# The values product of an attention block: three split passes per group, or 32-column strips in plain float32 for two groups at once

## The reference, cut to what matters

```python
q, k, v = ln(x) @ Wq.T + bq, ctx @ Wk.T + bk, ctx @ Wv.T + bv     # heads of 32 columns
scores = einsum('bhnd,bhmd->bhnm', q, k) / sqrt(32)
o = einsum('bhnm,bhmd->bhnd', softmax(scores), v)                 # the product that is changed
x = x + tanh(g_xattn) * (o @ Wo.T + bo)
h = ln(x) @ W1 + b1
act = relu(h + c * w_imag * sin(phase + 0.1 * h))                 # c: a constant per column
x = x + tanh(g_ffn) * (act @ W2 + b2)
```

## Time and profile before

| | |
|---|---|
| runs | 2210.45 us median (2209.47 to 2213.6) |
| the profiled execution, first to last instruction | 2210.9 us |
| PE busy in matmuls | 2162.8 us (98%), 10129 matmuls |
| values product in PE | 576 matmuls, 144.7 us busy |
| DVE, ACT, POOL busy | 66%, 55%, 18% |
| granted PE clock, mean of the span | 0.996 |

### The profile page before, as it was taken

One profiled execution on the slowest core, in us unless ns is written; L12 is line 12 of the kernel. 1 busy time (PEld: TensorE's weight loads), 2 busy tenths in 40 slices (PEclk: granted clock), 3 DMA queues, 4 the chain that ended last, 5 costly groups with the idle time before them and its releaser, 6 DMA issues.

```text
span 2210.9 us, 28991 instructions
## 1 busy us (share of the span) xinstructions
PE 2162.8 (98%) x10129; PEld 1797.9 (81%) x10129; DVE 1448.6 (66%) x2533; ACT 1212.1 (55%) x3571; POOL 403.2 (18%) x331
## 2 busy tenths in 40 slices
PE   8889999999999989999999999999999999999999
PEld 6778888888888867888888888888888888888887
DVE  4567776776776758656656666566566566665654
ACT  3477777777777746444454444444444444544443
POOL 4033433333343321101101001011011010010110
PEclk9989999999999999999999999999999999999999
DMA  7534444545544534313123123123131231231210
GB/s 225 184 70 116 109 106 112 130 103 111 128 106 109 128 129 115 77 50 65 59 56 77 58 58 76 58 39 76 42 74 57 58 77 58 58 77 58 39 39 19
DMA packets 402479, 186.92 MB, mean 85 GB/s; under 512 B 324292, under 2 KB 338985, under 8 KB 402335
## 3 DMA queue, kind: packets, MB, share of 16 engines
q1 hardware_dynamic: 400943, 184.41, 33.3%
q0 software_dynamic: 960, 0.64, 0.2%
q10 hardware_dynamic: 432, 0.04, 0.0%
HBM read 108.86 MB, written 59.38 MB: 76 GB/s over the span
## 4 chain that ended last, share of the span: by engine, by line
PE 61%; DVE 2%; ACT 1%; DMA 0%; issue 0%; ACTq 0%; DVEq 0%
PE pair_bank L56 30%; PE m_bank L56 30%; DVE w_split L1429 0%; DVE hidden L1463 0%; DVE turns L1459 0%; DMA w_chunk<-in_L_ffn_W_dram 0%; ACT relu L1389 0%; DVE sine L1456 0%; ACT hidden L1398 0%; ACT turns L1400 0%; DVE relu L1446 0%; DVE stats L180 0%; DVE x_in L205 0%; ACT sine L1405 0%; ACT w_split L1385 0%
## 5 line engine op out<-in xcount | busy, mean ns | idle before, releaser
L56 PE MATMUL pair_bank<-w_split,relu 128*128 128x512 f32 x3072 | 738.5, 389 | 4.6 <-DVE relu L1446 4.0
L56 PE MATMUL m_bank<-xT,w_split 128*128 128x512 f32 x3024 | 726.3, 389 | 0.0
L56 PEld LDWEIGHTS pair_bank<-w_split,relu 128*128 128x128 f32 x3072 | 576.3, 188 | 126.5 <-issue 4.8
L56 PEld LDWEIGHTS m_bank<-xT,w_split 128*128 128x128 f32 x3024 | 567.8, 188 | 117.6
L1405 ACT ACTIVATE sine<-turns 128x512 f32<-128x512 f32 x256 | 162.0, 633 | 393.7 <-DVE turns L1459 393.7
L1052 ACT ACTIVATE exps<-pair_bank,lowest 128x77 f32<-128x77 f32 x1024 | 318.7, 361 | 81.5 <-DVE lowest L1102 81.5
L1389 ACT ACTIVATE relu<-hidden 128x512 fp32r<-128x512 f32 x256 | 162.2, 633 | 329.7 <-PE m_bank L56 228.6
L1446 DVE SCALAR_TENSOR_TENSOR relu<-hidden,relu 128x512 fp32r<-128x512 f32 x256 | 181.5, 709 | 201.2 <-ACT relu L1389 201.2
L1463 DVE SCALAR_TENSOR_TENSOR hidden<-sine,sine_gain,hidden 128x512 f32<-128x512 f32 x256 | 197.0, 770 | 170.1 <-ACT sine L1405 170.1
L200 POOL TENSOR_TENSOR rstd<-var_eps,minus_half 128x4 f32<-128x4 f32 x32 | 38.3, 1196 | 1154.8 <-DVE var_eps L196 1154.8
L1052 ACT ACTIVATION_READ_ACCUMULATOR exps<-pair_bank,lowest 128x1 f32 x1024 | 248.6, 243 | 0.0
(11 more groups left out here) (123 smaller groups left out, 1896.2 us busy)
## 6 DMA issues: line engine op xcount, KB each, us to landing
x_in<-in_x_dram SPq DMA_DIRECT2D x16, 1024.0 KB, 5.5
residual<-in_x_dram SPq DMA_DIRECT2D x64, 256.0 KB, 2.8
xT<-x_in SPq DMA_DIRECT2D x256, 64.0 KB, 2.3
x_scratch<-residual SPq DMA_DIRECT2D x64, 256.0 KB, 2.4
x_in<-x_scratch SPq DMA_DIRECT2D x16, 1024.0 KB, 5.5
residual<-x_scratch SPq DMA_DIRECT2D x64, 256.0 KB, 3.6
out_dram<-residual SPq DMA_DIRECT2D x64, 256.0 KB, 2.1
quad_scratch<-x_in SPq DMA_DIRECT2D x60, 256.0 KB, 5.6
```

Source lines behind the costliest of these rows:

```text
L56: mm = pe.matmul(out, stationary(s), moving(m), start=first and n == 0, stop=last and n == len(PASSES) - 1)
```

## The change

The values product no longer uses hi and lo. The values are stored and loaded once, as float32. A transposed chunk of probabilities is copied by DVE alone into one float32 tile. Each head gets its own matmul: weights are the 128 x 32 columns of `v_diag` that belong to the head in that chunk, and the result goes to the head's own 32 partitions of the bank. A head's 77 rows fall into one or two chunks; over two groups every head has exactly three such pieces (`strips`). `value_products` issues the 12 pieces of two groups, step by step, the four heads in turn, at the end of the odd slots; the even slots have no values product. Operands are plain float32.

In the compiled program of the changed kernel each plain float32 piece stands as two pairs of a weight load and a matmul, one pair right behind the other (384 pieces, 768 matmuls; the 576 split ones are gone).

```diff
-        v_diag = sb(att, "v_diag", [P, 2, G // 2, 2, NC, P], F32R)
+        v_diag = sb(att, "v_diag", [P, 2, G // 2, NC, P])
...
+        for j in range(HG):
+            strip = []
+            for second in range(2):
+                of_head = [c for h, c, _, _, _ in pieces[second] if h == j]
+                strip += [(second, c, i == 0, i == len(of_head) - 1) for i, c in enumerate(of_head)]
+            strips.append(strip)
...
-                        sp.wait_ge(v_split, RT * r + j + 1)
+                        sp.wait_ge(v_summed, RT * r + j + 1)
...
-                    if not s.values_first:
-                        s.values = (*m.next(), h.next()[0]) if s.finish else None
+                    if s.finish and g % 2 == 1 and not s.values_first:
+                        s.values = [(*m.next(), h.next()[0]) for _ in range(2)]
...
-                        if s.finish and place != AFTER and g < 2:
-                            sp.wait_ge(m_full, s.values[0])
-                            load_values(sp, b, g, values_loaded[g])
+                        if s.values and place != AFTER and g == 1:
+                            sp.wait_ge(m_full, s.values[1][0])
+                            for second in range(2):
+                                load_values(sp, b, second, values_loaded[second])
...
-                    pe.wait_ge(m_split, n - 2)
-                    for c in range(NC):
-                        mm = matmul3(pe, m_bank[bank][:, :], lambda p: v_diag[:, g % 2, g // 2, p, c, :],
-                                     lambda p: probsT[p][:, g % 2 * (NC - 1) + c, :], c == 0, c == NC - 1)
-                    mm.then_inc(m_full, 1)
+                    pe.wait_ge(m_split, ns[1] - 2)
+                    for step in range(len(strips[0])):
+                        for j in range(HG):
+                            second, c, first, last = strips[j][step]
+                            mm = pe.matmul(m_bank[banks[second]][j * DH:(j + 1) * DH, :],
+                                           v_diag[:, second, pair, c, j * DH:(j + 1) * DH],
+                                           probsT[:, second * (NC - 1) + c, :], start=first, stop=last)
+                            if (step, j) in (ends[0], ends[1]):
+                                mm.then_inc(m_full, 1)
...
-                        if s.finish:
-                            for c in s.chunks:
-                                bank_hi(probsT[0][:, c, :], *s.probs[c])
...
-                def bank_lo(dst, hi, n, bank):
-                    dve.wait_ge(t_hi, n)
-                    dve.tensor_tensor(dst, t_bank[bank][:, :], hi.bitcast(F32), ALU.subtract).then_inc(t_split, 1)
+                def copy_probs(c, n, bank):
+                    dve.wait_ge(t_full, n)
+                    dve.tensor_copy(probsT[:, c, :], t_bank[bank][:, :]).then_inc(t_copied, 1)
...
-                            heads_lo(parity ^ (g < 2), s.back[1], *s.values[1:])
+                            for i, (_, bank, h) in enumerate(s.values):
+                                heads_lo(parity ^ (g < 2), s.back[1] - 1 + i, bank, h)
```

More of the change, by code:

```diff
@@ L268, in gated_attention_ffn_kernel @@
         PIECES = len(pieces[0])
+        strips = []
+        for j in range(HG):
[4 more added lines that the diff above has]
+            strips.append(strip)
+        assert all(len(strip) == len(strips[0]) for strip in strips)
+        ends = [max((step, j) for j in range(HG) for step, piece in enumerate(strips[j]) if piece[0] == second)
+                for second in range(2)]
         def load_keys(queue, b, g, loaded):
@@ L619, in values_sum @@
                         dve.wait_ge(v_full, RT * r + j + 1)
+                        if not (isinstance(r, int) and r == 0):
+                            dve.wait_ge(v_stored[j], 16 * r)
                         dve.tensor_tensor(v_sum[j][0:n, :], v_bank[j % 2][0:n, :], bv_rows[0:n, :], ALU.add)\
                            .then_inc(v_summed, 1)
[L623 to L628, removed]
                     steps = [0]
@@ L975, in scores, with value_products @@
                     mm.then_inc(scores_full, 1)
-                def value_product(b, g, n, bank, probs_split):
-                    pe.wait_ge(t_split, probs_split)
+                def value_products(b, pair, ns, banks, probs_copied):
+                    pe.wait_ge(t_copied, probs_copied)
                     if isinstance(b, int) and b == 0:
@@ L994, in block_output, with finish_pair @@
                     mm.then_inc(m_full, 1)
+                def finish_pair(s):
+                    of, g = s.back
+                    value_products(of, g // 2, [v[0] for v in s.values], [v[1] for v in s.values],
+                                   s.probs[s.chunks[-1]][0])
                 def turn(b, parity, place):
@@ L1024, in turn @@
                                 transpose_probs(*s.back, c, *s.probs[c])
-                        if s.finish and not s.values_first:
-                            value_product(*s.back, *s.values[:2], s.probs[s.chunks[-1]][0])
-                            last_heads = s.values[0]
+                        if s.values and not s.values_first:
+                            finish_pair(s)
+                            last_heads = s.values[1][0]
                     if place == AFTER:
@@ L1076, in turn @@
                             x_hi(1 - parity, range(HALF))
-                        if s.finish:
-                            n, bank, _ = s.values
+                        for i, (n, bank, _) in enumerate(s.values or ()):
                             act.wait_ge(m_full, n)
-                            act.activation(oT[parity ^ (g < 2)][0][:, s.back[1], :], m_bank[bank][:, :], ACT.Copy)\
+                            act.activation(oT[parity ^ (g < 2)][0][:, s.back[1] - 1 + i, :], m_bank[bank][:, :], ACT.Copy)\
                                .then_inc(m_hi, 1)
```

89 lines of the change are left out of this document (26 added, 63 removed).

## The result

The changed kernel took 2294.74 us (median of 4 runs, 2291.97 to 2296.42), the kernel before 2212.02 beside it: a ratio of 1.0379, 95% interval 1.0367 to 1.0392. The forecast was 2204, and its range ended at 2290. The profiled execution's span is 2291.9 us.

The account below looks back on a forecast made before the run. PE was taken to bound the kernel. A turn of 33.31 + 2 x 2.7 + 1.25 + 2.4 = 42.36 us against 42.74 saves 0.38; over 16 turns 6 us, giving 2204 us, range 2175 to 2290.

Parts of the forecast that it names:

- SP's queue: All 12 value loads behind slot 1 put the next x's load at 23.6 us, lengthening slot 3's wait by up to 0.95.
- the forecast's 2.4: Slot 3: PE's wait ahead of the pair for the queries' split, 2.4 us, between 1.8 and 2.75.
- the forecast's 0.6 for a late x: Slot 3: the part of the 2.4 us wait beyond 1.8, for x landing after DVE wants it.
- its 1.8 for ACT and DVE: Slot 3: PE waits 1.8 us, signal included, while ACT and DVE split the queries just produced.
- the clock: Rival: slot 3's wait lowers PE's granted clock, costing 20 to 40 us, about 2234 us; chance 0.09.
- the pair: Two groups' values products on PE: 24 issues, four at once, 6 x 0.40 + 0.3 = 2.7 us, two pairs a turn.
- two at a time: Rival: PE's strict order lets only two issues overlap, a pair takes 5.4 us, 2280 us in all; chance 0.31.
- one at a time: Rival: no overlap of strips, a pair takes 9.8 us, about 2420 us in all; chance 0.13.
- cheap issues: Rival: four issues at once at 0.232 us each, a pair takes 1.7 us, 2172 us in all; chance 0.09.
- The slot-1 wait: PE waits ahead of slot 1's pair for DVE's `gate_output`: 1.1 to 1.45 us, middle 1.25.
- the rest's +0.49: The turn's remaining PE work, without pairs and their waits: forecast 33.31 us, measured 33.80.
- nothing gained off PE: Work taken from ACT and DVE in attention is worth nothing by itself, since PE is busy 98.6 us of 100.

Follow-up runs that it names:

- e1: The changed kernel with scratch rows of the values 544 floats apart instead of 512: 2230.92 us, ratio 1.0093.
- e2: The changed kernel with SP loading the next x ahead of the twelve value loads, which keep the 512 pitch: 2229.85 us, ratio 1.0085.
- e5: e1 with 16 useless transposes of the identity on PE during its wait in slot 3: 2207.02 us, ratio 0.9984.
- e3: e1 with the pieces issued strip by strip, all three of one head before the next head's: 2299.03 us in one run.
- e7: e4 with, in slot 3, DVE splitting the queries before the sums and ACT making their high part after half of the first half's exponentials: 2210.69 us, ratio 0.9998.
- e4: e1 with the pair's first step waiting only for its own bank, the second step for the other: 2188.09 us, ratio 0.9898.

## Why the prediction was wrong

**The step that failed: SP's queue.** The forecast put "six more loads at 2.75 us per six" and x's load at 23.6 us after slot 1's start. The twelve took 11.06 us, and x's load came at 28.1. The price was taken from the rows of before, but the change also rewrites the source of these loads (values of a row side by side instead of grouped by head), so the trace of before had no row for them, and I gave them no bounds. The mechanism (x's load behind the value loads, the sums behind x, the queries' split behind the sums) is the one in the trace. This is 64 us of the 91 (after less e1).

That e1's wait of 2.31 meets the forecast's 2.4 is in part luck: with x ahead of the values (e2) it is 2.32 as well. At e1's issue time the forecast's 0.6 for a late x is almost nothing (DVE's sums wait 2.1 us for x in all of e1's attention, against 64.2 in the changed kernel), and its 1.8 for ACT and DVE is really 2.3, because ACT starts 0.66 us after PE has stopped and not at once.

**The second: the clock.** The forecast held it at 1.00 and kept its fall as a rival of chance 0.09, "about 2234". e1, with the forecast's wait, took 2230.9, and e5 showed the cause: 24 us. The rival's evidence was 3.00 us without work in setup; here 2.31 us was mostly enough. When a forecast creates a wait near one that is seen to cost clock, the fall belongs into the sum. How near is near stays open: after 2.31 to 2.46 us the pair was slow in 12 of 13 turns of e1, after 2.32 or 2.33 us in 10 of 13 of e2 and in 1 of 13 of e3, after 1.86 in 6 of 13 of e7, and after 3.39 us at attention's start (155.48 in the changed kernel) it was not, so the length of the wait alone does not decide it.

**Right: the pair and slot 1.** 2.71 us against 2.7, by 0.427 a round and 0.15 instead of 0.40 and 0.3. That ruled out two at a time (5.4 in the prediction; 13 x 0.40 + 0.3 is 5.5), one at a time (9.8) and cheap issues (1.7). Two at a time rested on strict order; it did not happen, although the two issues of one piece stand right behind each other. Of the chance of 0.59 for slower, 0.42 lay on these two rivals: that the kernel came out slower bears out the direction by luck, not by their mechanism. The Trainium skill, "TensorE: Matmul & The Clock Gate", section "Part 3: Packing small matmuls", states both program order in start and end and overlap of strips; the trace agrees with the second. e3's 5.33 us shows that order still matters. The Trainium skill, "FP8 and Floating Point Precision", section "TensorE Precision Notes", gives four passes for true float32; by the row of 0.232 a piece would cost an estimated 0.93 us, and the measured 2 x 0.427 = 0.85 is nearest to that. The slot-1 wait was 0.93 for 1.25: DVE was not late there, so the 0.15 that the middle held for that goes, and the rest of the gap is that the wait counts from the end of PE's last matmul and not from where the next one would have started. Part of the rest's +0.49 is this same time.

**Right: nothing gained off PE.** ACT is busy 1130.3 us instead of 1212.1, and the kernel is slower. That the copies would be cheaper was left open in the forecast; they are not.

## What to carry to other kernels

A DMA whose pattern is rewritten has no price in the trace of before: bound its issue time on its queue, and put loads that another engine waits for ahead of those that have time. A wait of PE can cost more than itself, since the work behind it may run at the lower clock (a wait of 2.31 us in e1 was followed by 4.41 us for a pair of 2.71); splitting the wait, so that a part of the work starts on what is ready, was worth 43 us here (e1 to e4), nearly as much as the cheaper product itself (8.37 - 2 x 2.71 us a turn, 47 us in all). By an estimate from the slow pairs of e1 and e4, some 20 of the 43 are the clock that no longer falls.

## What the runs showed of the hardware that was not expected

- The issue of a load took 817 ns on SP with scratch rows of 512 floats and 352 with 544 or 1024, for the same bytes; twelve of them in a row took 11.06 and 5.06 us. POOL's issues took 694 ns with 512 and with 544.
- Plain float32 strips of 32 columns run four at a time, 0.427 us a round of 512 columns, if the heads alternate; strip by strip the same 24 issues took 5.33 us instead of 2.71.
- 16 useless transposes in a wait made a kernel 24 us faster (e1 to e5), through the granted clock of the work after it, which went from 0.62 to 1.00. Waits as short as 1.86 us were followed by slow work, in 6 of 13 turns of e7.
